# Four-layer GNN megakernel: the last blocks of two products, and the first blocks after them, run node tile by node tile

## What is computed

```python
h = relu(layernorm(x)); x = x + attention(h, mask of the edges) @ wo.T + bo              # layer 0
h = relu(layernorm(x))                                                                 # layer 1
u = h @ root + bias + sum over 8 relations r of mean_r(h) @ weight[r]
z = concat(u, h) @ w_gate + b_gate
x = x + tanh(u) * z + h * (1 - z)
h = relu(layernorm(x))                                                                 # layer 2
m = relu(h @ W_self0 + mean(h) @ W_neigh0 + b0)
x = x + m @ W_self1 + mean(m) @ W_neigh1 + b1
h = relu(layernorm(x))                                                                 # layer 3
out = x + h @ W.T + bias          # W: the edge weights summed into a matrix, 384 x 384 of it used
```

## Time and profile before

| what | us |
|---|---|
| runs shown: median, lowest | 989.72, 989.1 |
| the profiled execution, its own time | 988.7 |
| its span from first to last instruction | 986.9 |
| mean granted TensorE clock | 0.974 |

### The profile page before, as it was taken

One profiled execution on the slowest core, in us unless ns is written; L12 is line 12 of the kernel. 1 busy time (PEld: TensorE's weight loads), 2 busy tenths in 40 slices (PEclk: granted clock), 3 DMA queues, 4 the chain that ended last, 5 costly groups with the idle time before them and its releaser, 6 DMA issues.

```text
span 986.9 us, 13646 instructions
## 1 busy us (share of the span) xinstructions
PE 934.6 (95%) x4743; PEld 823.6 (83%) x4743; DVE 614.1 (62%) x1001; ACT 368.8 (37%) x583; POOL 461.9 (47%) x413
## 2 busy tenths in 40 slices
PE   4999999998999789999999999999999959999994
PEld 4999999997889778888888888888888848878883
DVE  6998888867883525655656556565657366445535
ACT  6333333346883343222222322232243234244311
POOL 5324435455564450756547475474759003216212
PEclk8999999999999989999999999999999979999997
DMA  8998766542345364443453544543333603232301
GB/s 204 243 262 232 207 161 160 144 105 17 50 72 170 65 193 145 115 142 107 143 160 106 162 106 141 150 120 97 97 107 128 212 26 136 99 107 99 115 22 64
DMA packets 89796, 128.09 MB, mean 130 GB/s; under 512 B 34488, under 2 KB 67472, under 8 KB 89744
## 3 DMA queue, kind: packets, MB, share of 16 engines
q1 hardware_dynamic: 72640, 123.02, 41.8%
q0 software_dynamic: 15584, 0.11, 3.9%
q10 hardware_dynamic: 1520, 4.30, 1.2%
HBM read 116.65 MB, written 7.59 MB: 126 GB/s over the span
## 4 chain that ended last, share of the span: by engine, by line
PE 85%; DMA 6%; DVE 3%; POOL 3%; issue 2%; ACT 1%; SPq 0%; POOLq 0%; DVEq 0%; ACTq 0%
PE ps L609 48%; PE ps L437 20%; PE ps L656 8%; DMA count_d<-met,cell 4%; PE ps L554 2%; PE ps L527 2%; POOL count_d L1543 1%; PE ps L490 1%; PE ps L414 1%; DMA raw<-in_L_gnn_root 1%; DMA b_in<-in_L_gnn_bo 1%; DVE stats L1070 1%; PE ps L760 1%; PE ps L644 1%; DVE h L1422 0%
## 5 line engine op out<-in xcount | busy, mean ns | idle before, releaser
L1195 DVE TENSOR_TENSOR wlo<-raw,whi 128x1024 fp32r<-128x1024 f32 x120 | 204.3, 1705 | 141.9 <-ACT whi L845 141.8
L437 PE MATMUL ps<-acts,whi 128*128 128x384 f32 (+1 forms) x896 | 230.3, 338 | 0.0
L1573 POOL TENSOR_TENSOR mean_lo<-mean_f,mean_hi 128x384 fp32r<-128x384 f32 x80 | 92.4, 1155 | 196.2 <-ACT mean_hi L989 196.2
L437 PEld LDWEIGHTS ps<-acts,whi 128*128 128x128 f32 x896 | 161.8, 189 | 0.9 <-issue 0.5
L989 ACT ACTIVATE mean_hi<-mean_f 128x384 fp32r<-128x384 f32 x80 | 42.0, 525 | 299.0 <-DVE mean_f L1331 299.0
L437 PE MATMUL ps<-acts,wlo 128*128 128x384 f32 (+1 forms) x448 | 150.4, 336 | 0.0
L609 PE MATMUL ps<-whi,mean_hi 128*128 128x512 f32 x480 | 149.4, 392 | 0.0
L609 PE MATMUL ps<-whi,mean_lo 128*128 128x512 f32 x480 | 148.8, 391 | 0.0
L609 PE MATMUL ps<-wlo,mean_hi 128*128 128x512 f32 x480 | 148.6, 391 | 0.0
L845 ACT ACTIVATE whi<-raw 128x1024 fp32r<-128x1024 f32 x120 | 125.4, 1048 | 27.1 <-PE ps L609 21.7
L1594 POOL DMA_INDIRECT weight_d<-weight_sum,cell x48 | 95.8, 1996 | 30.7 <-DMA weight_d<-weight_sum,cell 19.3
(11 more groups left out here) (177 smaller groups left out, 1419.4 us busy)
## 6 DMA issues: line engine op xcount, KB each, us to landing
raw<-in_L_gnn_weight SPq DMA_DIRECT2D x64, 512.0 KB
rows_b<-rows_d SPq DMA_DIRECT2D x24, 384.0 KB, 5.2
raw<-in_L_gnn_w_gate SPq DMA_DIRECT2D x16, 512.0 KB
raw<-in_L_gnn_W_self SPq DMA_DIRECT2D x16, 512.0 KB
raw<-in_L_gnn_W_neigh SPq DMA_DIRECT2D x16, 512.0 KB
count_d<-total_r SPq DMA_DIRECT2D x8, 576.0 KB
rel_r<-count_d SPq DMA_DIRECT2D x8, 576.0 KB, 4.5
raw<-in_L_gnn_wq SPq DMA_DIRECT2D x32, 128.0 KB
```

Of the source, the lines that this page charges most:

```text
L437: mm = pe.matmul(ps[:, j % 2, 0:N], stationary[j % RING][:, k, :], acts[:, a, moving, k, :], start=i == 0, stop=i == 3 * KT - 1)
L1195: dve.tensor_tensor(wlo_row[slot], raw[slot][:, :], whi_row[slot].bitcast(F32), ALU.subtract)\
L1573: pool.tensor_tensor(mean[1][:, k % 2, :], mean_f[:, k % 2, :], mean[0][:, k % 2, :].bitcast(F32), ALU.subtract).then_inc(S["mean_lo"], 1)
```

## The change

- The last four blocks of T_GU and the last three of T_N0 and T_N1 run in `node_by_node`: all of them for node tile 0, then tile 1, then tile 2. In T_N1 the last tile runs half by half of its outputs.
- The first four blocks (`FIRST`) of the three `own_product`s also run node tile by node tile. `turn_tile` transposes four feature blocks of one node tile at once. Where these transposes stand is written out: `first_of` puts those of tile 0 (and 1) between the last blocks of the stage before.
- DVE and ACT are put in an order to match: tile 0 is normalised while tile 1 is still summed. `row_low` and `row_high` of the next weights stand between.
- In `own_product`, `row_low` and `row_high` of tiles 4 to 7 now follow the transposes of the same block.
- Neighbour means have three places instead of two, as three of them are needed at once.
- `sum_planes`: POOL adds the three count planes, one matmul with ones stays in `start_relation`. The counts share the buffer `inv`.
- The shift of the norm is a tensor_scalar instead of a scalar_tensor_tensor.
- In the last layer each tile is transposed, split and multiplied on its own; the output stores stand in the order in which they become ready.

```diff
+            def turn_tile(y, source, nt, blocks=FIRST):
+
+                need(pe, S["turn_lo"], y - 1)
+                for k in range(blocks):
+                    mm = pe.transpose(ps[:, 6 + y % 2, P * k:P * k + P],
+                                      source[:, nt, P * k:P * k + P], ident[:, :])
                 mm.then_inc(S["turned"], 1)
 
...
+            def node_by_node(t, blocks, between, halves=False):
+
+                for nt in range(NT):
+                    if halves and nt == NT - 1:
+                        for f in range(2):
+                            for t_k, stationary, k, ready in blocks:
+                                for a, weight in ((0, whi_row), (0, wlo_row), (1, whi_row)):
+                                    mm = pe.matmul(ps[:, 2 * nt + f, :], stationary[a][:, k, P * nt:P * nt + P],
+                                                   weight[t_k % RING][:, HALF * f:HALF * f + HALF], start=False,
+                                                   stop=t_k == t + len(blocks) - 1 and a == 1, skip_group_check=True)
+                                if f:
+                                    mm.then_inc(S["w_used"], 1)
+                            if f == 0:
+                                mm.then_inc(S["half_ready"], 1)
+                                between(nt, 0)
+                        return
+                    for n, (t_k, stationary, k, ready) in enumerate(blocks):
+                        if nt == 0:
+                            pe.wait_ge(S["w_lo"], t_k + 1)
+                            ready()
+                        mm = row_tile(t_k, t_k % RING, stationary, k, nt, last=n == len(blocks) - 1)
+                        if nt == NT - 1:
+                            mm.then_inc(S["w_used"], 1)
+                            between(nt, n)
+                    if nt < NT - 1:
+                        mm.then_inc(S["sum_ready"], 1)
+
             def start_relation(q, edges, ready, a6):
 
 
                 a6()
                 ready()
-                for s in range(NT):
-                    mm = pe.matmul(ps[:, 6, 0:N], ones_r[:, :], edges[:, s, :], start=s == 0, stop=s == NT - 1)
+                pe.wait_ge(S["planes_made"], R + 1 if isinstance(q, int) and q > R else q + 1)
+                mm = pe.matmul(ps[:, 6, 0:N], ones_r[:, :], planes[:, :], start=True, stop=True)
                 mm.then_inc(S["agg_ready"], 1)
...
+            def own_product(t0, y0, source, q, edges, ready, ahead):
+
+                h0 = H_ALL[max(q - R + 1, 0)]
+                rest = y0 + NT - FIRST
+                units = {(0, -1): 0, (1, -1): 1, (2, -1): 2}
+                if ahead:
+                    units = {(0, 1): 1, (1, 2): 2} if ahead == 1 else {(0, 1): 2}
+
+                def unit(nt):
+                    pe.wait_ge(S["h_ready"], h0 + nt + 1)
+                    turn_tile(y0 + nt, source, nt)
+
+                for nt in range(NT):
+                    if (nt, -1) in units:
+                        unit(units[nt, -1])
+                    pe.wait_ge(S["turn_lo"], y0 + nt + 1)
+                    for k in range(FIRST):
+                        pe.wait_ge(S["w_lo"], t0 + k + 1)
+                        mm = row_tile(t0 + k, k % RING, h_t, k, nt, first=k == 0)
+                        if nt == NT - 1:
+                            mm.then_inc(S["w_used"], 1)
+                        if (nt, k) in units:
+                            unit(units[nt, k])
+                        if nt == NT - 1 and k % 2 == 0:
+                            pe.wait_ge(S["h_ready"], H_ALL[max(q - R + 1, 0) + 1])
+                            turn(rest + FIRST + k // 2, source, FIRST + k // 2)
+                for k in range(FIRST, KT):
                     if k == KT - 1:
                         pe.wait_ge(S["row_lo"], (q - R + 1) * NT + NT if q >= R else NT)
-                        start_relation(q, edges, ready, lambda: pe.wait_ge(S["turn_lo"], y0 + KT))
-                    pe.wait_ge(S["turn_lo"], y0 + k + 1)
-                    row_block(t0 + k, k % RING, h_t, k, first=k == 0,
-                              bank_free=first_free if k == 0 else None)
+                        start_relation(q, edges, ready, lambda: pe.wait_ge(S["turn_lo"], rest + KT))
+                    pe.wait_ge(S["turn_lo"], rest + k + 1)
+                    row_block(t0 + k, k % RING, h_t, k)
                     if k + 2 < KT:
-                        turn(y0 + k + 2, source, k + 2)
+                        turn(rest + k + 2, source, k + 2)
 
             def relation(q, t0, edges, last, following=None, ready=None):
...
+            def last_relation(q, t0, edges, between, halves=False):
+
+                def block(k):
+                    return t0 + k, [mean_of(q, k, a) for a in range(2)], 0, lambda: aggregated(q, k)
+
+                for k in range(KT - 3):
+                    sum_edges(q, edges, k + 1)
+                    if k == KT - 4:
+                        sum_edges(q, edges, k + 2)
+                    aggregated(q, k)
+                    row_block(t0 + k, k % RING, [mean_of(q, k, a) for a in range(2)], 0)
+                sum_edges(q, edges, KT - 1)
+                node_by_node(t0 + KT - 3, [block(k) for k in range(KT - 3, KT)], between, halves)
+
             slots = [rel_r[:, i, :, :] for i in range(2)]
...
-                if k < KT - 2:
-                    row_block(T_GU + k, k % RING, u_t, k)
-            last_two_blocks(T_GU + KT - 2, (u_t, KT - 2), (u_t, KT - 1), lambda: None)
-
-
-            y0 = begin(1)
+                row_block(T_GU + k, k % RING, u_t, k)
+
+            def first_of(q, y0, at):
+
...
+                        pe.wait_ge(S["h_ready"], H_ALL[q] + at[nt, n] + 1)
+                        turn_tile(y0 + at[nt, n], h, at[nt, n])
...
+                return lambda: pe.wait_ge(S["turn_lo"], Y_U + k + 1)
+
...
-            own_product(T_S0, y0, h, R, total_r, lambda: None)
-            relation(R, T_N0, total_r, True)
-            y0 = begin(2)
...
+            own_product(T_S1, Y_MID, h, R + 1, total_r, lambda: None, 2)
+
+            def first_turned(nt, n):
+                pe.wait_ge(S["agg_read"], (KT + 1) * (R + 2))
+                pe.wait_ge(S["h_ready"], H_ALL[3] + 1)
+                turn_tile(Y_H3, h, 0, NT)
+
+            last_relation(R + 1, T_N1, total_r, first_turned, True)
+
+
+            pe.wait_ge(S["h_ready"], H_ALL[3] + 2)
+            turn_tile(Y_H3 + 1, h, 1, NT)
             pe.wait_ge(S["w3_lo"], 1)
             for nt in range(NT):
-                i = 0
-                for k in range(NT):
-                    for a, w in ((0, 0), (0, 1), (1, 0)):
...
                 dve.wait_ge(S["std_ready"], NT * n + nt + 1)
                 link(dve.reciprocal(rstd[:, nt, :], std[:, nt, :]))
-                dve.scalar_tensor_tensor(shift[:, nt, :], mv[:, nt, 0:1], -1.0, rstd[:, nt, :], ALU.mult, ALU.mult)\
+                dve.tensor_scalar(shift[:, nt, :], mv[:, nt, 0:1], rstd[:, nt, :], -1.0, ALU.mult, ALU.mult)\
...
             def own_product(n, t0, q):
-                for k in range(KT):
-                    row_low(t0 + k + 2, (k + 2) % RING)
-                    if k + 2 < KT:
-                        turned_low((Y_H1, Y_H2, Y_MID)[n] + k + 2, h_t[1][:, k + 2, :], h_t[0][:, k + 2, :])
+                rest = (Y_H1, Y_H2, Y_MID)[n] + NT - FIRST
+                for k in range(FIRST, KT):
+                    turned_low(rest + k, h_t[1][:, k, :], h_t[0][:, k, :])
+                    low_at(t0 + k)
+                low_at(t0 + KT)
+                low_at(t0 + KT + 1)
                 read_counts(q)
                 read_sums(q, 0)
...
                     read_counts(q + 1)
                     read_sums(q + 1, 0)
 
+            def last_relation(q, t0, more):
+
+                for k in range(KT - 1):
+                    if k < KT - 2:
+                        low_at(t0 + k + 2)
+                    read_sums(q, k + 1)
...
             own_product(1, T_S0, R)
-            relation(R, T_N0, True)
+            last_relation(R, T_N0, True)
             dve.wait_ge(S["brow_in"], 16 * 3)
-            add_bias(2, T_S1 - 1, h, "mid_ready")
-            turned_low(Y_MID, h_t[1][:, 0, :], h_t[0][:, 0, :])
-            turned_low(Y_MID + 1, h_t[1][:, 1, :], h_t[0][:, 1, :])
+            add_bias(2, T_S1 - 1, h, "mid_ready", (0, 1))
+            tile_turned_low(Y_MID, 0)
+            low_at(T_S1 + 1)
+            low_at(T_S1 + 2)
+            tile_turned_low(Y_MID + 1, 1)
+            add_bias(2, T_S1 - 1, h, "mid_ready", (2,))
+            low_at(T_S1 + 3)
+            tile_turned_low(Y_MID + 2, 2)
             own_product(2, T_S1, R + 1)
             dve.wait_ge(S["w3_hi"], 1)
             dve.tensor_tensor(w3[1][:, :, :], mask[:, :, :], w3[0][:, :, :].bitcast(F32), ALU.subtract)\
                .then_inc(S["w3_lo"], 1)
-            relation(R + 1, T_N1, True)
+            last_relation(R + 1, T_N1, False)
 
             dve.wait_ge(S["x_based"], NT)
```

(31 more changed lines are left out.)

299 lines of the change are left out of this document (190 added, 109 removed).

## The result

The changed kernel takes 966.3 us (median of four runs), the kernel before 989.5 beside it: ratio 0.977, 95% interval 0.975 to 0.979. Forecast: 963.85 us, range 957 to 975. One of the four runs of the kernel before took 1886.3 us and does not count in the ratio. Of 25.85 us expected, 23.2 came by these medians; between the two profiled executions (988.7 and 966.0 us) it is 22.7. The span of the latter is 964.3 us.

A forecast was written before the change was run, and what follows sets the result against it. PE (TensorE), busy 95% of the span, was taken as the bound. 3.5 + 0.5 + 11.3 + 0.05 + 10.5 = 25.85 us off 988.7 gave 962.85, plus 1.0 for the median 963.85 us; range 957 to 975.

The forecast's parts named there:

- A: Edge counts in `start_relation`: one matmul instead of three, POOL's sums hidden; 0.35 us ten times, 3.5 us gained.
- C: Gate product to next product: 12.6 us recoverable, 1.3 us lost in small waits; 11.3 us gained, bounds 12.6 and 6.
- E: End of the program, last neighbour matmul to last matmul: 19.9 us falls to 9.4; 10.5 us gained, bounds 9.0 and 11.9.
- D: First neighbour product to second product: 4.4 us recoverable, less 0.75 and 3.6 lost; gain 0.05 us, bounds -1.95 and +4.4.
- B: First product of the graph stage: PE resumes root block 4 earlier; 0.5 us gained, bounds 0 and 1.6 us more.
- two cases: Second product's count reading: PE waits 1.6 us if VectorE keeps its turn, 5.6 us if `wlo` and POOL's additions alternate.
- T: In the end stage, the moment when the last neighbour product's matmuls end on PE; the prediction had 964.1 us before.
- D's start: Join behind the first neighbour product: hole and slow block recovered, less 0.75 us of small waits; 3.65 us gained.
- DVE as the bound at the joins: Rival: per-tile normalising slips in the queue shared with weight halves, PE stalls per tile; 15 us gained, 974.6 us, chance 0.18.
- The slower case by `planes_made`: Rival at each relation's start: POOL's scatter waits for its DMA, PE waits for the plane sums; near 1001 us, chance 0.04.
- Plane sums lose: Rival in the relations: POOL's additions push `mean_lo` or `wlo` 0.7 us past PE's need; 5.6 us lost, 969.3 us, chance 0.10.
- The signs: Expected in the trace: PE's waits for `h` from 23.8 to under 4 us; clock below 1 in the last few matmuls.

## Why the prediction was right

The forecast, 963.85, is 2.4 us under the measured 966.3, which lies inside the forecast's band of 960 to 968. The mechanisms of A, C and E are shown, that of A by an experiment, C's by the filled stretches of both traces, E's by them and in part by two experiments. But the sum came out close partly by luck: D was wrong by 4.7 us, C and A by 0.75 and 1.0 the same way, and B and E made up 1.7 each. Between profiled executions the miss is 3.1 us; the 1.0 I added for the median was 0.3 here, which hid 0.7 of it.

- **D failed.** Forecast 0.05, bounds -1.95 and +4.4; measured -4.65 (2.6 at its start, -7.25 at its end), beyond the lower bound. The failed step is "I take the middle, 3.6: D = 4.4 - 0.75 - 3.6 = 0.05 us". My two cases differed by whether `wlo` and addition alternate; they do: counts read at 906.06, 37.7 us behind the first neighbour product's end at 868.37, where I had 37.5 for that case. Taking the middle of two cases of which only one can happen was the first mistake. The second: I gave the wait no clock. PE waited 0.69 + 3.54 = 4.2 us (I had 5.6), and the block behind cost 6.62 - 4.12 = 2.5 more; 0.34 of the 7.25 are tile 0's transposes of the last layer, which moved ahead of T; the blocks behind holes had cost 1.6 and 1.8 more in the earlier trace rows. The lower bound lacked it too. The eight traces with a hole of 3.5 us behind a wait of 0.35 to 0.7 for `inv` show 6.51 to 7.18 us for the block, 2.4 to 3.1 more; without the wait for `inv` (the row work one tile earlier) it was 5.96. The third: I named the order of the `wlo` as the cause, and moving one back changed nothing. What is shown is that the additions beside them did it: moving these away took 6.0 us off this stretch. Why they stand there is argued: GpSimd's row work starts 7.5 us nearer to the counts, since ScalarE's `row_parts` went from behind block 3's transposes to behind block 5's.
- By the rule of the Trainium skill that I quoted ("SBUF — State Buffer", who interferes with whom), GpSimd goes between the `wlo`, and that case it was. The trace agrees: single additions took 3.38 us for 2.4, and the second and third `wlo`, which stood beside them, 3.42 and 3.41 for 1.23. I had read the rows of before as speaking for neither.
- **D's start and C.** 2.6 us for 3.65, and 10.55 for 11.3 (81.75 less 79.16 and 158.14 less 147.59, the stretches of the run with three counts). In each, 0.7 us is a PE wait for block 6's `wlo`, which took 3.5 us beside `h_row_lo`; I had that clash only for `xres`. The waits I did list came smaller: 0.38 us for the second block's `wlo` (0.6 forecast), 0.16 at the neighbour join (0.55). The 0.7 us waits went away when the row work moved. What else is missing is some tenths at the changes between transposes and matmuls; I haven't placed it.
- **B** gave 2.2 us; "Gain 0.5 us" took the low side. The reversed order did as said, and more: no hole is left at root block 4 (0.5 us at most), and the clock doesn't fall there. That is about the upper bound I gave, 0.5 + 1.6. In executions whose last scatter started as late as before (352.4), at 352.6 to 353.1, it is 1.1 to 1.8, so a part of the 2.2 is chance.
- **A** gave 2.5 for 3.5, 0.34 us per relation where GpSimd's sums are hidden. The cover that "just fits" fell short in relation 7, relation 0 gave half, and the last product's share went into the wait for VectorE.
- **E** gave 12.2 for 10.5. The term that was mis-sized: "So 9 at 0.32 and 9 at 0.17: T + 9.4". All matmuls of the end ran at 0.17 us; I had carried the half clock over from holes of 3.3 and more, and here PE's longest pause was 1.5 us. That takes off 1.35; the chain itself was 0.5 shorter than T + 8.0, and the 19.9 of before is 19.7 by the same landmark. The bound of 9.0 should have been 9.2 by its own terms. The shift's form was right as forecast. The rule of the Trainium skill, same page and section, by which tensor_scalar can contend as well, did not apply on one column: 0.21 us beside an addition of 2.36.
- **The rivals.** DVE as the bound at the joins is refuted: the gate stretch of 11.6 us has 11.22 of PE work. The slower case by `planes_made` never showed a wait. "Plane sums lose" held for one relation of eight, with 0.43 us.
- **The signs.** Two came out otherwise: the waits for `h` are 5.3 us and not under 4, and the granted clock is 1.00 behind the last neighbour product and not below 1.

## What to carry to other kernels

When a change moves a step earlier or later on PE, ask for each helper engine how far ahead of its deadline its work now starts; here GpSimd work that nobody waited for directly came to stand beside VectorE's and cost some 6 us. VectorE and GpSimd instructions that lengthen each other add their work up: count the sum of both from the start of the pair, and put the one without a deadline where the other is idle. Price each PE hole with the slower block behind it, and give exclusive cases chances, not a mean.
